# Weight loads, pick tables, weight folds and two steps of the scan put in another order in a Mamba-2 block with a mixture of experts

## The reference

```
h = rmsnorm(layernorm(x)) ; proj = h @ w_in_proj            # 128 -> 1544: z, x, B, C, dt
x = silu(causal_conv4(x)) ; dt = mean_head(softplus(dt @ w_dt + b_dt))
y = chunked scan over chunks of tokens, 8 heads, state 64:   # M = exp(l_i - l_j) below the diagonal
    y_c = (M * (C B^T)) x + exp(l) C state ; state = exp(l_end) state + (decayed B)^T x
out = residual + rmsnorm((y + x*D) * silu(z)) @ w_out_proj
f = layernorm(x1) ; weights = top2(softmax(f @ gate_w + gate_b))
x2 = x1 + mean over 2 shared experts relu(f W1 + b1) W2 + b2 + weighted routed experts (4, top 2)
```

## Time and profile before

| what | us |
|---|---|
| median of 3 executions | 692.43 (684.56, 692.43, 693.63) |
| the profiled execution, whole | 693.27 |
| its span in the profile | 691.6 |
| TensorE busy | 620.6 (90%) |
| VectorE busy | 456.8 (66%) |
| ScalarE busy | 361.0 (52%) |
| GpSimd busy | 184.3 (27%) |

### The profile page before, as it was taken

One profiled execution on the slowest core, in us unless ns is written; L12 is line 12 of the kernel. 1 busy time (PEld: TensorE's weight loads), 2 busy tenths in 40 slices (PEclk: granted clock), 3 DMA queues, 4 the chain that ended last, 5 costly groups with the idle time before them and its releaser, 6 DMA issues.

```text
span 691.6 us, 12143 instructions
## 1 busy us (share of the span) xinstructions
PE 620.6 (90%) x4098; PEld 461.3 (67%) x4098; DVE 456.8 (66%) x1120; ACT 361.0 (52%) x793; POOL 184.3 (27%) x241
## 2 busy tenths in 40 slices
PE   3977789998999899988999899988999889997996
PEld 2655667666776677766676766766777666766764
DVE  5777666766686676656867666766766667654453
ACT  2754466536754467527565276535675275642341
POOL 7074103421152112430134111521134201341002
PEclk9999899999999999999999999999999999998799
DMA  8000000000100001000000001000010000000000
GB/s 252 9 17 1 1 0 16 1 1 1 31 1 1 1 0 32 1 1 0 13 17 0 0 0 30 0 0 0 0 30 0 0 2 16 1 1 2 15 1 15
DMA packets 12728, 8.90 MB, mean 13 GB/s; under 512 B 1642, under 2 KB 11284, under 8 KB 12692
## 3 DMA queue, kind: packets, MB, share of 16 engines
q1 hardware_dynamic: 12048, 8.27, 4.0%
q10 hardware_dynamic: 644, 0.17, 0.2%
HBM read 6.33 MB, written 2.10 MB: 12 GB/s over the span
## 4 chain that ended last, share of the span: by engine, by line
PE 34%; DVE 22%; issue 14%; ACT 9%; POOL 8%; DVEq 0%; POOLq 0%; ACTq 0%
PE bank L361 6%; DVE act_l L1204 4%; PE bank L363 4%; PE bank L362 4%; ACT decay L830 3%; PE bank L587 3%; ACT act_h L806 3%; POOL CTe L1410 3%; PE bank L588 2%; PE bank L589 2%; POOL decay L1424 2%; PE bank L530 2%; PE bank L521 2%; POOL rs L1351 1%; DVE cv L1042 1%
## 5 line engine op out<-in xcount | busy, mean ns | idle before, releaser
L1204 DVE SCALAR_TENSOR_TENSOR act_l<-bank,act_h 128x512 fp32r<-128x512 f32 x192 | 131.5, 689 | 150.4 <-ACT act_h L806 148.5
L806 ACT ACTIVATE act_h<-bank 128x512 fp32r<-128x512 f32 x192 | 117.2, 610 | 154.2 <-PE bank L363 151.4
L361 PE MATMUL bank<-fTl,w1h 128*128 128x512 f32 x192 | 92.4, 481 | 17.8 <-DVE act_l L1204 10.2
L1433 POOL TENSOR_TENSOR late<-late 128x512 f32<-128x512 f32 x32 | 46.6, 1455 | 225.4 <-DVE late L1212 225.4
L587 PE MATMUL bank<-act_l,w2h 128*128 128x512 f32 x192 | 79.0, 411 | 6.0 <-DVE late L1212 5.4
L830 ACT ACTIVATE decay<-bank,lneg 128x128 f32<-128x128 f32 x256 | 69.8, 388 | 20.2 <-PE bank L456 20.2
L363 PE MATMUL bank<-fTh,w1h 128*128 128x512 f32 x192 | 77.2, 402 | 0.0
L362 PE MATMUL bank<-fTh,w1l 128*128 128x512 f32 x192 | 77.2, 402 | 0.0
L588 PE MATMUL bank<-act_h,w2l 128*128 128x512 f32 x192 | 76.3, 397 | 0.0
L589 PE MATMUL bank<-act_h,w2h 128*128 128x512 f32 x192 | 76.2, 397 | 0.0
L1420 POOL TENSOR_TENSOR xw<-xs,decay 128x128 f32<-128x128 f32 x48 | 19.5, 407 | 180.5 <-ACT decay L830 122.1
(11 more groups left out here) (192 smaller groups left out, 1182.6 us busy)
## 6 DMA issues: line engine op xcount, KB each, us to landing
x_in<-L_attn_hidden_dram SPq DMA_DIRECT2D x8, 256.0 KB, 2.9
out_dram<-late SPq DMA_DIRECT2D x8, 256.0 KB, 2.8
late<-L_ffn_sw_dram SPq DMA_DIRECT2D x2, 512.0 KB, 8.8
late<-L_ffn_rw_dram SPq DMA_DIRECT2D x1, 1024.0 KB, 9.4
CT<-L_attn_w_in_proj_dram SPq DMA_DIRECT2D x1, 772.0 KB, 6.9
b_dt<-L_attn_b_dt_dram ACTq DMA_DIRECT2D x1, 128.0 KB, 5.3
w_out_raw<-L_attn_w_out_proj_dram SPq DMA_DIRECT2D x1, 128.0 KB, 6.0
d_col<-L_attn_D_dram SPq DMA_DIRECT2D x8, 0.1 KB, 2.8
```

The costliest lines, as they stand in the source:

```text
L361: mm(dst, stat_h, mov_l, start=True, stop=False)
L806: nc.scalar.activation(act_h[:, b % RING, :], HID[b % 2][:], ACT.Relu).then_inc(act_h_ready, 1)
L1204: v_.scalar_tensor_tensor(act_l[:, r, :], HID[b % 2][:], 0.0, f(act_h[:, r, :]), ALU.max, ALU.subtract)\
L1433: g.tensor_tensor(acc, acc, term, ALU.add).then_inc(acc_ready, 1)
```

## The change

1. SyncE waits for the projection weights before it issues the FFN weights.
2. The pick tables are built as one-hot tables of 24 x 8 and 12 x 4 by six affine selects, and spread to 24 x 1024 and 12 x 512 by two copies with a broadcast input. GpSimd does its memsets before the first `rsqrt1`.
3. A fold is two functions, `fold_weights` (the 512-column matmul) and `fold_bias` (the four others), placed apart between the steps of scan 0; fold 1 leaves the place before `lcs`. VectorE's `w1_parts` are spread over the chunks in another way (0; 1; 2 and 3; 4).
4. In the opening the fourth C projection stands behind `l_transposes`, ACT makes the B and C high parts behind hTh, and VectorE the low part of z before hTl and those of B and C apart.
5. In every pass, the transposes of the next input stand behind the y product of chunk 2 (place 20), hTh at place 20 on ACT, and hTl at place 20 on VectorE.
6. In every `scan_end`, the output product is made chunk by chunk and stands before the last `sum_squares`.

```diff
@@ sync
             sp_eng.dma_start(w_out_raw[:], a["w_out_proj"].rearrange("(b p) o -> p b o", p=P)).then_inc(small_in, 16)
+            sp_eng.wait_ge(win_in, 16)
             sp_eng.dma_start(wf_raw[:, 0, 0:2, :], a["sw1"].rearrange("n d f -> d n f")).then_inc(wf1_in, 16)
@@ tensor
-            def out_projection(s):
-                pe.wait_ge(mg_ready, nth(s, 8, 8))
-                pe.wait_ge(yz_ready, nth(s, 4, 4))
-                for c in range(NCH):
-                    for b in range(NB):
-                        ins = mm(MAIN[2][:, at(c)], yT[:, b, at(c)], w_out[:, b, :], start=(b == 0), stop=(b == NB - 1))
-                ins.then_inc(o_psum, 1)
+            def out_projection(s, c):
+                if c == 0:
+                    pe.wait_ge(mg_ready, nth(s, 8, 8))
+                pe.wait_ge(yz_ready, nth(s, 4, c + 1))
+                for b in range(NB):
+                    ins = mm(MAIN[2][:, at(c)], yT[:, b, at(c)], w_out[:, b, :], start=(b == 0), stop=(b == NB - 1))
+                if c == NCH - 1:
+                    ins.then_inc(o_psum, 1)
...
-            def fold_bias(g):
+            def fold_weights(g):
                 if g == 0:
                     pe.wait_ge(wf1_in, 2 * 16)
-                    pe.wait_ge(cols_set, 2)
                 if g > 1:
                     pe.wait_ge(w1l_set, g - 1)
-                dst = HID[g % 2]
-                mm(dst[:], center[:], wf_raw[:, 0, g, :], start=True, stop=False)
+                mm(HID[g % 2][:], center[:], wf_raw[:, 0, g, :], start=True, stop=False)
+
+            def fold_bias(g):
+                if g == 0:
+                    pe.wait_ge(cols_set, 2)
                 for k in range(NF):
...
@@ tensor, scan_part
                         if c < NCH - 1:
                             b_tokens(s, c)
-                        elif not is_seq(s, n_seq - 1):
-                            hn_transposes(s + 1)
...
                     if step == 2:
                         y_product(s, c)
+                        if c == NCH - 2 and not is_seq(s, n_seq - 1):
+                            hn_transposes(s + 1)
@@ tensor, scan_end
                     proj(s + 1, 1)
+                for c in range(NCH):
+                    out_projection(s, c)
                 sum_squares(s, NCH - 1)
-                out_projection(s)
@@ tensor, opening
                 proj(0, 7)
+                fold_weights(0)
                 fold_bias(0)
...
                 x_tokens(0, 1)
-                fold_bias(1)
                 lcs(0, None, None)
-                for j in (10, 11, 12, 13):
-                    proj(0, j)
+                proj(0, 10)
+                proj(0, 11)
+                proj(0, 12)
                 l_transposes(0)
-                for i in range(CHUNKS_FROM, NBLK):
-                    c, step = divmod(i - CHUNKS_FROM, 3)
-                    scan_part(0, None, None, i)
-                    if step == 1:
-                        fold_bias(2 + c)
+                proj(0, 13)
+                for c in range(NCH):
+                    segments(0, c)
+                    if c < NCH - 1:
+                        b_tokens(0, c)
+                    gram(0, c, None)
+                    fold_weights((1, 3, 4, 5)[c])
+                    if c < NCH - 1:
+                        growth_rows(0, c + 1)
+                    else:
+                        proj(1, 0)
+                    fold_bias((1, 2, 4, 5)[c])
+                    y_product(0, c)
+                    if c == 0:
+                        fold_weights(2)
+                    if c == 1:
+                        fold_bias(3)
+                    if c == NCH - 2:
+                        hn_transposes(1)
@@ scalar, scan_part and opening
                         decays(s, c)
-                        if c == NCH - 1 and not is_seq(s, n_seq - 1):
-                            hT(s + 1)
...
+                    if step == 2 and c == NCH - 2 and not is_seq(s, n_seq - 1):
+                        hT(s + 1)
...
                 w_high(Z0, 0, DI)
-                w_high(B0, 512, 512)
-                w_high(C0, 1024, 512)
                 act.wait_ge(wdt_psum, 1)
                 nc.scalar.copy(wh[:, DT0:DT0 + DI], MAIN[2][:, 0:DI]).then_inc(wdth_set, 1)
                 hT(0)
+                w_high(B0, 512, 512)
+                w_high(C0, 1024, 512)
@@ vector, body and opening
-                            if i == NBLK - 3:
+                            if i == NBLK - 4:
                                 hT_low(s + 1)
...
+                w_low(Z0, 0, DI, 2)
                 hT_low(0)
-                w_low(Z0, 0, DI, 2)
-                w_low(B0, 512, 1024, 4)
+                w_low(B0, 512, 512, 3)
+                w_low(C0, 1024, 512, 4)
...
-                        if c == 0:
-                            w1_parts(0)
-                        w1_parts(c + 1)
+                        for n in ((0,), (1,), (2, 3), (4,))[c]:
+                            w1_parts(n)
@@ gpsimd, opening
+                for t, v in ((ident_bf, 0.0), (ones, 1.0), (upto, 1.0), (turn, 0.0), (one_head, 0.0),
+                             (one_expert, 0.0), (lower, 1.0), (center, -1.0 / P)):
+                    g.memset(t[:], v).then_inc(zeros_set, 1)
                 rsqrt1(0)
...
-                for t, n, v in ((pick_head, NH, 1.0), (pick_expert, NE, 1.0)):
+                for t, n in ((one_head, NH), (one_expert, NE)):
                     for part in range(3):
-                        g.affine_select(out=t[:], in_=t[:], pattern=[[-1, n], [0, P]], compare_op=ALU.not_equal, fill=v,
+                        g.affine_select(out=t[:], in_=t[:], pattern=[[-1, n]], compare_op=ALU.not_equal, fill=1.0,
                                         base=-part * n, channel_multiplier=1).then_inc(tables_set, 1)
...
+                g.tensor_copy(pick_head[:], one_head[:].unsqueeze(2).to_broadcast([3 * NH, NH, P])).then_inc(tables_set, 1)
+                g.tensor_copy(pick_expert[:], one_expert[:].unsqueeze(2).to_broadcast([3 * NE, NE, P])).then_inc(tables_set, 1)
```

More of the change, by code:

```diff
@@ L82, in build @@
         pick_expert = sb("pick_expert", [3 * NE, NE, P], BF16)
+        one_head = sb("one_head", [3 * NH, NH])
+        one_expert = sb("one_expert", [3 * NE, NE])
         lower = sb("lower", [P, NE, NE])
@@ L379, in proj @@
                 pe.wait_ge(hTl_ready, nth(s, 1, 1))
-                if is_seq(s, 0) and j in (2, 4, 6):
-                    pe.wait_ge(weights_set, j // 2 + 1)
+                if is_seq(s, 0) and j in (2, 6):
+                    pe.wait_ge(weights_set, 2 if j == 2 else 5)
                 if j == 1 and not is_seq(s, 0):
@@ L428, in lcs @@
                 if is_seq(s, 0):
-                    pe.wait_ge(tables_set, 11)
+                    pe.wait_ge(tables_set, 13)
                 pe.wait_ge(dt_steps, nth(s, 3, 3))
@@ L596, in fold_gate @@
                 mm(TR[:, 0:NE], center[:], gw[:], start=True, stop=True).then_inc(gfold_psum, 1)
+            def fold_weights(g):
+                if g == 0:
+                    pe.wait_ge(wf1_in, 2 * 16)
+                if g > 1:
+                    pe.wait_ge(w1l_set, g - 1)
+                mm(HID[g % 2][:], center[:], wf_raw[:, 0, g, :], start=True, stop=False)
             def fold_bias(g):
                 if g == 0:
-                    pe.wait_ge(wf1_in, 2 * 16)
                     pe.wait_ge(cols_set, 2)
-                if g > 1:
-                    pe.wait_ge(w1l_set, g - 1)
-                dst = HID[g % 2]
-                mm(dst[:], center[:], wf_raw[:, 0, g, :], start=True, stop=False)
                 for k in range(NF):
                     b = g * NF + k
-                    ins = mm(dst[:, at(k)], b1_mean[:, b:b + 1].to_broadcast([P, P]), ident[:], start=False, stop=k == NF - 1)
+                    ins = mm(HID[g % 2][:, at(k)], b1_mean[:, b:b + 1].to_broadcast([P, P]), ident[:], start=False, stop=k == NF - 1)
                 ins.then_inc(fold_psum, 1)
@@ L1361, in opening @@
                                 channel_multiplier=1).then_inc(tables_set, 1)
+                for t, v in ((ident_bf, 0.0), (ones, 1.0), (upto, 1.0), (turn, 0.0), (one_head, 0.0),
+                             (one_expert, 0.0), (lower, 1.0), (center, -1.0 / P)):
+                    g.memset(t[:], v).then_inc(zeros_set, 1)
                 rsqrt1(0)
-                for t, v in ((ident_bf, 0.0), (ones, 1.0), (upto, 1.0), (turn, 0.0), (pick_head, 0.0),
-                             (pick_expert, 0.0), (lower, 1.0), (center, -1.0 / P)):
-                    g.memset(t[:], v).then_inc(zeros_set, 1)
                 pool.wait_ge(zeros_set, 12)
```

## The result

The changed kernel takes 668.4 us (median of 5, 668.36 to 669.86), the kernel before beside it 692.44 (median of 5): a ratio of 0.968, 95% interval 0.962 to 0.973. Its profiled execution took 668.36 us, span 666.6.

A forecast was written before the change was run, and what follows sets the result against it. It took the kernel as a ring of hand-overs, bounded by which wait ends last at each. Opening 5.1, sequences 6.9, last sequence -1.3 and clock 2.5 gave 13.2 us off 693.3: 680, range 673 to 689.

The forecast's parts named there:

- Part 5: Clock at sequence ends: filling TensorE's 0.99 us idle makes half-clock drops rarer, worth 2.5 us.
- I count half of the 5.1: Clock step: drops ending sequences 0, 3, 4 and 6 cost 5.1 us; half, 2.5 us, taken as won.
- rival B: Clock drops just as often, at other places: 682.6 us, or 688 with a drop in each further sequence; chance 0.14.
- Part 1: Next input's transposes in sequences 0 to 6: hTl ready earlier, 1.1 us each, bounds 0.4 and 1.5.
- behind it VectorE still has a low part and two conv taps: After the mg multiply: this VectorE work (0.6 + 1.3 us) holds yT, leaving a 1.1 us gain.
- Part 2: Output product before last sum: about zero alone, add released by rstd; last sequence loses 1.27 us.
- Part 3: Opening: moved folds, projection and conversions bring the first add earlier, worth 5.1 us, bounds 2.5 and 6.5.
- Part 4: Edits at nothing: FFN loads behind the projection weights, pick tables by copies, reordered high and low parts; 0 us.
- C: Rival: all of it, the full 5.1 us of clock and 6.5 in the opening, 676 us; chance 0.16.
- A: Rival: VectorE takes it back, middle sequences gain 0.4 us and the opening 2.5; 687 us; chance 0.17.
- D: Rival: output products ahead of the last sum delay rstd, all 1.79 us on the path; 700 us; chance 0.03.
- E: Rival: moved work is hidden anyway, loop unchanged, only the opening gains; 688 us; chance 0.05.

The follow-up runs named there:

- filled4: Kernel before plus 4 unread matmuls in TensorE's idle ahead of the last sum of squares, not in the last sequence; 687.3 us, ratio 0.995.
- both_loop: Kernel before with the moved transposes, hTh and hTl and the output product ahead of the last sum, old opening kept; 673.8 us, ratio 0.976.
- undo_wait: Changed kernel without SyncE's wait, so the FFN loads are issued at once as before; 669.5 us.
- after_again: Changed kernel itself, unaltered, measured again on the same chip as the version with the last sum between output chunks; 669.7 us.
- undo_folds: Changed kernel with whole folds at their old places and VectorE's conversions in their old order; 671.2 us.

## Why the prediction was wrong

The 24.9 us of span between the two profiled executions split into 5.0 of opening, 10.5 of passes, -1.2 at the last and 10.6 of clock; forecast were 5.1, 6.9, -1.3 and 2.5.

**Part 5, the clock, was mis-sized: 10.6 us instead of 2.5.** Without half clock (as in filled4) pass 1 and the four loop passes of the kernel before are 1.0 + 3.9 = 4.9 shorter, add 0 had 1.4 in it, and the tail gave 4.3. Two steps failed. "I count half of the 5.1": the loss at the ends of sequences went whole, 1.4 + 3.9 = 5.3, and pass 1 gave 1.0 more. And the tail stood in the sum at nothing, without a reason, though rival B named its two drops. No edit touches the tail's code, yet its time moves with the granted clock:
```profile
626.00:686.00 60.00, 52.31 (x199) 37.59 (x197) 30.49 (x70) 20.82 (x36) 6.15 (x5) 0.89 0.02 5
```
```profile
606.00:662.00 56.00, 44.73 (x190) 31.85 (x190) 30.31 (x70) 19.95 (x35) 7.42 (x6) 1.00 0.02 6
```
These are the kernels before and after. The tail took 60.9 us with no half clock before the last output (after), 62.0 to 62.1 with 6.8 (both_loop, undo_wait, after_again), and 65.1 to 65.2 with 13.7 (before, filled4, undo_folds). What decides between them no run shows; the same kernel got 0 and 6.8 (after, after_again). Up to 4 of the 24 us are thus luck, and some of it is in the median: three of its five executions were granted 0.994 of the clock and took 668.4, where four of the six of after_again, 669.7 in the median, were granted 0.987 to 0.991.

**Part 1 was right in kind and too small.** 1.15 per pass was forecast; 1.5 was measured in passes 1 and 2 (75.35 to 73.82, 79.03 to 77.52) and 1.9 in the four loop passes (79.57 to 77.68 on the mean). The step that failed is "behind it VectorE still has a low part and two conv taps". The low part of the earlier trace rows's chunk did not follow the multiply at once in the kernel before:
```profile
218.63 0.69 DVE L1204 SCALAR_TENSOR_TENSOR act_l<-bank,act_h 128x512 fp32r<-128x512 f32 x1 [0.52 <-ACT act_h L806]
```
It waited 0.52 for the relu, and that wait went with TensorE's start, so VectorE passed on 1.44 to 1.49 instead of 1.1. The other 0.4 per loop pass is not explained: in the kernel before a loop pass is 0.5 longer than pass 2, in the kernel after 0.2.

**Part 2 was right:** zero in the middle (a tenth less), -1.2 in the last, and the releaser as forecast. **Part 3 was right in sum, in part by luck:** 5.0 with the clock left out (5.1), the add at 67.25 (67.15). The segments of chunks 0 and 1 came 0.7 and 0.8 early, at 30.8 and 38.0 (31.5, 38.8), and those of chunk 3 at 55.1 (55.0), since chunks 1 and 2 took 8.1 and 9.1 us where 7.8 and 8.4 were forecast. Chunk 2 became longer than its 8.6 before:
```profile
48.85 2.44 DVE L1041 TENSOR_SCALAR hn<-x_in,mv,rs 128x128 f32<-128x128 f32 x4
...
52.55 0.43 PE L515 MATMUL bank<-mg,xs 128*32 128x128 f32 x8 [0.54 <-DVE mg L1118]
```
The sum by rows had 1.1 for hn, and it took 2.44 for the four, 332 to 1323 ns each as before; TensorE waited for the multiply behind it. The rule of the Trainium skill weighed there (SBUF — State Buffer, Who interferes with whom) agrees with this trace: it stood for up to 2.8. The longest, 1323 ns, started at 49.72 beside GpSimd's CTe (49.69, for 1.27). By that rule the opening would be worth 4; without the 0.8 us by which chunk 1 began early it would have been 4.2. How much of the 0.7 in chunk 2 is hn's no run separates. **Part 4 was right as far as settled:** the copy into pick_head took 1.03 us (1.1 taken), the tables are worth nothing, and SyncE's wait stays open. The FFN loads landed 5.7 to 6.3 us after their issue, sooner than before.
```profile
10.03 1.03 POOL L1405 CAST pick_head<-one_head 24x1024 bf16<-24x1024 f32 x1
```
At the one place where a rule of the Trainium skill (TensorE: Matmul & The Clock Gate, Part 1) spoke against the change, the trace agrees with it: 2.69 us idle at add 0, and a granted clock of 0.57 over the four microseconds that follow, so mostly 1.2 GHz. It cost nothing there, as the passes above show. Of the rivals C came nearest (676), still short, since it too left the tail alone; A, B as a whole, D and E did not happen.

## What to carry to other kernels

An idle microsecond on TensorE can cost more by the clock that falls behind it than by itself: 0.99 us stood idle, and an end at half clock was 1.1 to 1.6 us longer. Look up the granted clock at each place of a repeated pattern, and before reordering real work, fill the idle with unread matmuls that fit into it: over several executions it shows what the clock is worth. What half clock costs depends on the place, so take it from passes with and without it. When two kernels are compared by a per cent, compare the time between marks inside them too, for a stretch that no edit touches can move by 4 us, and compare the granted clock of all executions, for one profile is one draw.

## What the runs showed of the hardware

The drops at the ends of sequences are a tendency with chance in it. The profiles of the kernel before and of its copy begun two memsets later lost the clock at the same four ends, 0, 3, 4 and 6, though the ends look alike in their rows (the same sums, an idle of 0.99 or 1.05); yet over 48 executions the kernel before was granted anything from 0.968 to 0.992 of the clock. With four unread float32 matmuls (eight records, 1.05 us) in the idle of 0.99 us no end dropped in the profile, and no execution was granted less than 0.983.

A stretch of 3.4 us at half clock cost 1.1 to 1.6 us at an end (the passes to adds 3, 4 and 6, 81.19, 80.75 and 80.61, against 79.57, 79.59 and 79.50 in filled4) and nothing behind add 0.

Idle alone does not tell. In the tail an idle of 3.17 us in the kernel after was followed by whole clock, while the same idle of the same kernel in after_again lay beside half clock (608.4 to 615.2); in the kernel before 1.94 us were followed by half:
```profile
609.00 0.50 PE L364 MATMUL bank<-fTl,w1h 128*128 128x512 f32 x1 [3.17 <-DVE act_l L1227]
```
```profile
609.27 0.79 PE L364 MATMUL bank<-fTl,w1h 128*128 128x512 f32 x1 [3.18 <-DVE act_l L1227]
```
```profile
629.63 0.50 PE L361 MATMUL bank<-fTl,w1h 128*128 128x512 f32 x1 [1.94 <-DVE act_l L1204]
```
